# A state-space stage run by sequence inside a stage of indirect gathers

## The reference

```python
sx, ix = top_k(sim[0], 8); sy, iy = top_k(sim[1], 8)         # 128 keys each
scores, pk = top_k((sx[..., :, None] + sy[..., None, :]).reshape(..., 64), 8)
indices = take_along_axis(ix[..., :, None] * 128 + iy[..., None, :], pk)
w = silu(einsum('btd,bthkd->bthk', x, down_embed[indices])) * softmax(scores)
y = einsum('bthk,bthkd->btd', w, up_embed[indices])
y = y + (silu(x @ Wg.T) * (x @ Wu.T)) @ Wd.T
```

```python
u, v = split(x @ in_proj_w + in_proj_b)
v = depthwise_conv3(silu(v)) + conv_b
h_t = a * h_{t-1} + ssm_b * v_t;  y_t = ssm_c * h_t + ssm_d * v_t      # a = sigmoid(logit_a)
out = (u * silu(y)) @ out_proj_w + out_proj_b
part = layernorm(out + x) * ln_w + ln_b
```

## Time and profile before

| what | value |
|---|---|
| median of 3 runs | 3108.74 us (3105.13 to 3114.55) |
| the profiled execution: span | 3106.5 us; no other time is given for it |
| gather stage | from 1879 to 2595 us, gathers from 1898.4 to 2577 |
| its layer norm | 2595 to 2617 us |
| state-space stage with both norms | 2617 to 2730 us |
| busy over the span | PE 75%, DVE 52%, ACT 31%, POOL 25% |

### The profile page before, as it was taken

How to read it: one execution, slowest core, us unless ns; L and a number is a source line. 1 busy time by engine, 2 the same in 40 slices (tenths; PEclk the granted TensorE clock), 3 DMA queues, 4 the chain that set the end, 5 groups by cost and what they waited for, 6 DMA issues and landing times. The chain is left out here.

```text
span 3106.5 us, 37880 instructions
## 1 busy us (share of the span) xinstructions
PE 2320.2 (75%) x13729; PEld 1493.0 (48%) x13729; DVE 1607.0 (52%) x4352; ACT 963.3 (31%) x1784; POOL 787.0 (25%) x755
## 2 busy tenths in 40 slices
PE   6877699888777655485677674877777877689786
PEld 3544378735443432462244333666666664237332
DVE  3754300067545657246374666655665544533486
ACT  0132222210241322132114463443334334424343
POOL 1000200041001006451000004777777771000000
PEclk9999699989998877796899897988889889899898
DMA  7200244337006142553500106222222221000000
GB/s 183 63 21 2 99 149 172 143 85 177 11 18 176 38 159 108 182 179 128 94 5 23 69 1 152 66 55 56 53 55 58 62 53 37 0 29 1 1 0 27
DMA packets 126828, 232.20 MB, mean 75 GB/s; under 512 B 38777, under 2 KB 76537, under 8 KB 122560
## 3 DMA queue, kind: packets, MB, share of 16 engines
q1 hardware_dynamic: 73552, 125.12, 14.2%
q0 software_dynamic: 51952, 100.65, 11.0%
q10 hardware_dynamic: 1152, 4.19, 0.3%
HBM read 245.59 MB, written 66.72 MB: 101 GB/s over the span
## 5 line engine op out<-in xcount | busy, mean ns | idle before, releaser
L3192 POOL DMA_INDIRECT L2f_G<-in_L2f_table,L2f_idx x512 | 523.7, 1023 | 288.7 <-issue 155.2
L3249 PE MATMUL psum<-L2f_G,L2f_diag 128*128 128x256 f32 x1024 | 304.4, 463 | 168.8 <-ACT L2f_diag L3319 168.8
L3249 PEld LDWEIGHTS psum<-L2f_G,L2f_diag 128*128 128x128 f32 x1024 | 235.9, 236 | 234.8 <-ACT L2f_diag L3319 192.0
L3427 DVE CUSTOM_DVE_ANT_0 L2f_junk<-L2f_G,L2f_X 128x256 bf16<-128x256 f32 x512 | 182.8, 421 | 254.0 <-DMA L2f_G<-in_L2f_table,L2f_idx 253.9
L3319 ACT ACTIVATE L2f_diag<-const,L2f_actd 128x128 f32<-128x128 f32 x528 | 161.1, 388 | 24.2 <-DVE L2f_actd L3441 24.2
L1191 PE MATMUL psum<-constb 128*128 128x256 bf16 x512 | 81.0, 282 | 96.8 <-ACT L1a_PT L1358 24.6
L2669 POOL DMA_INDIRECT picks_x<-L1f_rows,L1f_put x64 | 71.0, 1109 | 242.1 <-ACT L1f_rows L2759 223.2
L3226 PE MATMUL psum<-xT,L2f_mw 128*128 128x256 f32 x512 | 123.2, 385 | 0.0
L3312 ACT ACTIVATE L2f_actd<-L2f_dots 128x9 f32<-128x9 f32 (+1 forms) x64 | 13.5, 211 | 316.3 <-DVE L2f_dots L3427 316.3
L1358 ACT ACTIVATE L1a_PT<-psum 128x1536 f32<-128x1536 f32 x32 | 46.4, 1450 | 205.5 <-PE psum L1326 205.5
L1191 PEld LDWEIGHTS psum<-constb 128*128 128x128 bf16 x512 | 41.0, 99 | 142.2 <-ACT L1a_PT L1358 32.9
(11 more groups left out here) (689 smaller groups left out, 4882.8 us busy)
## 6 DMA issues: line engine op xcount, KB each, us to landing
L1f_we<-in_L1f_w SPq DMA_DIRECT2D x32, 384.0 KB, 8.2
picks_x<-zeros SPq DMA_DIRECT2D x16, 544.0 KB, 9.1
L1f_xe<-picks_x SPq DMA_DIRECT2D x32, 272.0 KB, 2.9
picks_y<-zeros SPq DMA_DIRECT2D x16, 512.0 KB, 6.4
L2f_G<-in_L2f_table,L2f_idx POOLq DMA_INDIRECT x512, 2.8
slots_x<-zeros POOLq DMA_DIRECT2D x8, 512.0 KB, 7.6
L1f_wb<-in_L2x_w SPq DMA_DIRECT2D x1, 4096.0 KB, 12.2
L1f_g<-picks_y ACTq DMA_DIRECT2D x8, 512.0 KB, 11.9
```

The source lines that it names most:

```text
L3192: nc.gpsimd.indirect_dma_start(out=G[:, h, k, :], out_offset=None, in_=ins["L2f_table"], in_offset=bass.IndirectOffsetOnAxis(ap=IDX[:, t, ...
L3249: mm = nc.tensor.matmul(ps[:, MIX_BANK + t % 2, 0:D], diag[:, i % 2, k, :], row[:, D:2 * D], start=(h == 0 and k == 0), stop=(h == HEADS - ...
L3427: e = V.tensor_tensor_reduce(out=junk[:, k, :], in0=row[:, 0:D], in1=X[:, t % 3, :], scale=1.0, scalar=0.0, op0=ALU.mult, op1=ALU.add, acc ...
```

## The change

The stage L3a is no longer a stage. peer_ssm_stage takes peer_stage's place and runs it within the steps:

- The layer norm after L2f, the state-space part, its own norm and the layer norm after it are done for one sequence of 256 tokens at a time, in eight hops d = 0 to 7 (ssm_at). PE and ACT do hop d of sequence m at the end of step 9 + 8m + d, DVE one step later. The loop has END = 74 steps; the last ten have no gathers. Hop 0 subtracts the mean, 1 ends the L2f norm, 2 is conv, scan and skip, 3 the gate, 4 the output projection and residual, 5 the own norm, 6 and 7 the layer norm. All hops share PSUM bank 7; the dense MLP's down projection moves into one bank.
- Of a step's eight picks, the last two (OWN = 6) are weighted and summed on DVE into `rest`; ACT makes two diagonals and PE two matmuls fewer. keep, now on DVE, adds `rest` to the mix. POOL's wait before a head has a second part, pk_scaled.
- ACT's tables are named by hand (tables()) and loaded before the wait of the function that needs them.
- The squares of the norms are taken on DVE in place of ACT; the state-space input is projected in two hops (v in 2, u in 3); the skip product is on DVE in place of ACT.
- In best_pairs four additions become one; in experts 16 instructions of 64 elements become two of 512.
- ACT waits at the stage's start for the L3a weights and takes the sigmoid of logit_a. The weights of L3x are loaded by SP once pk_used shows the picks of step 60.

```diff
-STAGES = [..., "L2f", "L3a", "L3x", "L3f"]
+STAGES = [..., "L2f", "L3x", "L3f"]
...
+    def turned(i):
+        return [(k, row) for k, row in enumerate(rows(i)) if not OWN <= k < TOPK]
+    def ssm_at(i):
+        m, d = divmod(i - PER - 1, PER)
+        return (m, d) if 0 <= m < B else (0, None)
...
# POOL, before the gathers of a head
     pool.wait_ge(s["pk_used"].sem, s["pk_used"].at((t - 1) * HEADS + h + 1))
+    pool.wait_ge(s["pk_scaled"].sem, s["pk_scaled"].at((t - 1) * HEADS + h + 1))
...
# PE, a step
-                for i in range(STEPS):
+                for i in range(END):
                     up(i + 1); queries(t + 2); picks(i); down(i - 1); similar(t + 2); turn_back(t - 1)
+                    ssm(i)
...
# ACT
+                def inverse_root(done):
+                    tables(LOGS)
+                    act.wait_ge(s["var_ready"].sem, s["var_ready"].at(done))
+                    link(nc.scalar.activation(root, ps[:, SSM, 0:CW], ACT.Ln, bias=c.eps))
+                    link(nc.scalar.activation(root, root, ACT.Exp, scale=-0.5))
+                    nc.scalar.activation(square, root, ACT.Square).then_inc(s["root_ready"].sem, 1)
...
# DVE
+                def scaled(i):
+                    for k in range(OWN, TOPK):
+                        row, by = rows(i)[k][:, D:2 * D], act_d[:, i % 2, k:k + 1]
+                        if h == 0 and k == OWN:
+                            e = VE.tensor_scalar(rest[:, :], row, by, None, ALU.mult)
+                        else:
+                            e = VE.scalar_tensor_tensor(rest[:, :], row, by, rest[:, :], ALU.mult, ALU.add)
...
+                    if d == 2:
+                        for k in range(DH):
+                            link(VE.scalar_tensor_tensor(L[:, k, :], V[:, k, 1:1 + SEQ], cw(1), L[:, k, :], ALU.mult, ALU.add))
+                            link(VE.scalar_tensor_tensor(L[:, k, :], V[:, k, 2:2 + SEQ], cw(2), L[:, k, :], ALU.mult, ALU.add))
+                            VE.tensor_tensor_scan(H[:, k, :], decay[:, k:k + 1].broadcast_to([P, SEQ]), L[:, k, :], 0.0, ALU.mult, ALU.add)
+                            link(VE.tensor_scalar(S[:, k, :], L[:, k, :], wa["sd"][:, k:k + 1], None, ALU.mult))
+                            VE.scalar_tensor_tensor(S[:, k, :], H[:, k, :], both[:, k:k + 1], S[:, k, :], ALU.mult, ALU.add)
...
# DVE, a step
                     dot(i); add_mix(t - 1); add_dense(t // 2 - 1); gated(i); weighted(i)
+                    keep(t - 1); scaled(i)
+                    ssm(i - 1)
                     (best_keys, best_pairs, experts)[h - 1](t + 2)
...
-        norm_stage(nc, c, name, acc)
```

More of the change, by code:

```diff
@@ L3163, in peer_stage, with sa @@
         h_ = sb("h", [P, 3, CW])
-        mix = sb("mix", [P, 1, D])
+        mix, rest = sb("mix", [P, 1, D]), sb("rest", [P, D])
         got = ("got_head0", "got_head1", "got_head2", "got_head3")
+        def sa(nm, shape):
+            return work.enter_context(nc.sbuf_tensor(f"L3a_{nm}", shape, F32))
+        V = sa("V", [P, DH, SEQ + 2])
+        L, H, S, U = (sa(k, [P, DH, SEQ]) for k in ("L", "H", "S", "U"))
+        decay, both, mid = sa("a", [P, DH]), sa("both", [P, DH]), sa("mid", [P, DH + 1])
+        root, square, step = V[:, 0, 1:1 + SEQ], V[:, 1, 1:1 + SEQ], S[:, 0, :]
         def tile(t):
@@ L3215, in similar @@
                             rows = slice(half * RD, (half + 1) * RD)
-                            mm = nc.tensor.matmul(ps[:, SIM_BANK + half, tile(o_)], q[rows, o_, :],
+                            mm = nc.tensor.matmul(ps[:, SIM + half, tile(o_)], q[rows, o_, :],
                                                   w["keys"][rows, o_ * KEYS:(o_ + 1) * KEYS], start=True, stop=True)
@@ L3255, in turn_back, with average @@
                     for j in range(DH):
-                        mm = nc.tensor.transpose(ps[:, MIX_BANK + t % 2, tile(j)], mix[:, 0, tile(j)], c.ident)
+                        mm = nc.tensor.transpose(ps[:, MIX + t % 2, tile(j)], mix[:, 0, tile(j)], c.ident)
                     mm.then_inc(s["pk_yturn"].sem, 1)
+                def average(y):
+                    for j in range(DH):
+                        mm = nc.tensor.matmul(ps[:, SSM, 0:CW], c.mean, y[:, j, :], start=(j == 0), stop=(j == DH - 1))
+                    return mm
@@ L3328, in _ @@
+                c.wait_weights(act, "L3a")
+                nc.scalar.activation(decay[:, :], wa["la"], ACT.Sigmoid).then_inc(s["decay"].sem, 1)
                 for t in range(2):
@@ L3340, in _ @@
                         evac_queries(t + 2)
-                    if h == 0 and t:
-                        keep(t - 1)
                     if h == 0 and t + 2 < NT:
@@ L3458, in _ @@
                     experts(t)
-                for i in range(STEPS):
+                for i in range(END):
                     t, h = divmod(i, HEADS)
-                    dot(i)
-                    if h == 1 and t:
+                    if i < STEPS:
+                        dot(i)
+                    if h == 1 and 0 < t <= NT:
                         add_mix(t - 1)
@@ L3465, in _ @@
                             add_dense(t // 2 - 1)
-                    gated(i)
-                    weighted(i)
+                    if i < STEPS:
+                        gated(i)
+                        weighted(i)
+                    if h == 0 and 0 < t <= NT:
+                        keep(t - 1)
+                    if i < STEPS:
+                        scaled(i)
+                    ssm(i - 1)
                     if t + 2 < NT and h:
                         (best_keys, best_pairs, experts)[h - 1](t + 2)
-                add_mix(NT - 1)
-                add_dense(NT // 2 - 1)
+                    if i == 0:
+                        prepare()
                 s["dve_chain"].base += link.n
@@ L3518, in program @@
         run = STAGES
-        packed = [n for n in run if n in PACK]
+        packed = PACKED
         c.w, order = {}, {}
```

558 lines of the change are left out of this document (238 added, 320 removed).

## The result

The changed kernel takes 3026.14 us (median of 4 runs, 3024.55 to 3033.36), the kernel before 3110.72 beside it on the same chip (4 runs, 3105.13 to 3114.55): ratio 0.9732, 95% interval [0.971, 0.9754]. 3030 was forecast, with 3008 to 3050 as its own range. The profiled execution has a span of 3022.7 us, 83.8 less than before.

The account below looks back on a forecast made before the run. POOL's chain of gathers was taken to bound the gather stage. 3106.5 - 94 - 2 + 1 + 13 + 3 = 3027.5 us of span, so 3030 forecast (73%), own range 3008 to 3050, whole range 3006 to 3072.

Parts of the forecast that it names:

- the tail: After the last picks, before the cross-attention stage: 44.5 us in place of 138.5, so -94 us; over 55 would show it wrong.
- the spacing of the gathers: Sign, in the gather steps: gathers stand 1.33 to 1.36 us apart if the forecast is right.
- VectorE's wait for rows: Sign, in the gather steps: VectorE's wait for gathered rows falls from 254 us to 20 to 100.
- The hops' term: In the tail, eight hops in series: 38 us, with 33.5 at full clock and 42 as ends.
- the lead-in: Start of the tail: keep, then hops 6 and 7 of sequence 6, with hand-overs: 6.5 us.
- The table load in hop 5: In the tail, ScalarE's shift of xT and table load ahead of the root: 1.1 us not hidden by TensorE's matmul.
- The gathers: Gather steps: 129 us of added two-input VectorE work slows POOL's gathers by 0.10 us per us, +13 us.
- Rival 2: Gather steps: POOL and VectorE exclude each other, added two-input work costs +129 instead of +13, kernel 3146 us; chance 5%.
- VectorE's room: Gather steps: VectorE goes from 52 to 74 us a sequence, plus 3 to 8 of waits: 77 to 82 of 85.
- Rival 1: At weighted() after hops 1, 3, 5, 7: VectorE becomes the bound, 91 us a sequence against 85, kernel 3062 us; chance 22%.
- The start: Stage start: ScalarE's wait for L3a weights and sigmoid table +2, first tile's index arithmetic 1 shorter: +1 us in sum.
- Step 63: Last gather step: +3 us for ending later behind the gathers, and 2 us earlier for fewer matmuls and diagonals.

Follow-up runs that it names:

- Experiments 6 to 8: Changed kernel plus three idle TensorE matmuls before tail waits, 3021.55 us; then ScalarE's table loaded early too, 3023.35; then idle matmul counts fitted, 3150.33 on another chip.
- experiments 2 and 4: Changed kernel plus two unused 512-element VectorE instructions a step: two-input tensor_tensor, 3066.86 us; tensor_scalar, 3043.47 us.
- experiments 2 and 3: Changed kernel plus two unused 512-element VectorE instructions a step: two-input tensor_tensor, 3066.86 us; one-input reductions, 3065.01 us.
- experiment 5: Changed kernel with all eight picks of a step on TensorE: 3047.29 us, ratio 0.9778; the changed kernel beside it 3029.67 us.
- experiment 11: Changed kernel with TensorE running all eight picks' matmuls while ScalarE builds six diagonals: 3173.46 us, on a chip where the kernel before takes 3233.66.
- experiment 8: Changed kernel with early table load and idle TensorE matmuls fitted to each tail wait: 3150.33 us, ratio 0.9761, where the kernel before takes 3233.66.

## Why the prediction was right, step by step

The span was to shrink by 79 us and shrank by 83.8. The mechanism held; that the sum came so near is in part luck, since the tail missed by +3.8 us and the other terms by -8.6 together, of which 1.9 lie ahead of the stage. Of the signs, the spacing of the gathers (1.35 us) was in its range, VectorE's wait for rows (102) just above its 20 to 100, the last stretch 48.2 and not 45, and the first gather earlier, not later.

**The tail.** -94 was forecast, -90.2 came. That the norm, the state-space stage and its norms leave the path, and a lead-in and eight hops stay, held. The hops' term was mis-sized: 38 us, midway between 33.5 at full clock and 42 at 1.2 GHz, and it was 40.5 (2606.3 to 2646.8), the lead-in 7.7 for 6.5. On the path TensorE has four averages of 2.05 to 2.08 us, one of 1.13, and 3.78 and 3.52 for projection and output product; by these times all stood at 1.2 GHz but the one of 1.13 and a part of the output product. Experiments 6 to 8 show that this is the clock and nothing else in those matmuls, since the same instructions take 1.10 to 1.13 and 1.99 behind idle matmuls. The table load in hop 5, of which 1.1 us were taken as on the path, had 1.04 on it (2633.83 less 2632.79, the average's end).

**The gathers.** +13 forecast, +10.4 came; the price of 0.10 us for each us of two-input work was of the right size: 0.05 to 0.09 from the two picks, 0.13 from the two-input instructions against the one-input ones, and 8.3 us of the gathers' busy time for the hops' some 80 us (1 sequence's 18 less the picks' 6.7, times seven), 0.10. The forecast took the hops times eight, though those of sequence 7 lie behind the last gather: 1 us too much. It chose 0.10 among 0, 0.06 and 0.2, and that choice was a guess from one pair of gathers. Rival 2 falls with this: it needed 0.7. The Trainium skill ("SBUF - State Buffer", section "Who interferes with whom") has the loser block fully, lists tensor_scalar among the operations that can enter a two-port mode, and adds that a probe saw tensor_copy but not tensor_tensor stall such DMAs; experiments 2 and 4 show about a tenth of the time with tensor_tensor, and with tensor_scalar nothing above one-input work.

**VectorE's room.** 74 us a sequence and 3 to 8 of waits were forecast. Both came: in each of the sequences 2 to 6, from first dots to first dots, less the waits for rows and for weights, VectorE is taken for 73.9 to 74.1 us, and it waits 2.7 to 5.0 for the weights. Sequence 0, in whose steps no hop runs, has 60.0, so that the mean over all eight (577 us from first to last dots less 102, waits of 3.3 in it) is 69. Rival 1, VectorE as bound at 3062, was not far: experiments 2 and 3 reach 3067 and 3065 with 11 us more a sequence, and show its place, weighted(), and one of its signs, POOL waiting for picks.

**The start.** +1 forecast, -0.7 came. The sigmoid's table was loaded at 1877.21, ahead of the wait for the weights, not behind: the queries were copied 4.66 us after the stage began, for 4.26 before, +0.4 instead of +2.

**Step 63.** +3 for a later end and -2 for fewer matmuls were taken; -1.1 came. The last picks end 14.8 us after the last gather's start before the change, 12.9 with the hops left out, 13.8 and 13.4 with them: the 2 us for fewer matmuls were right, and of the 3 the hops cost 0.5 to 0.9.

**What the forecast didn't see** is that the two picks on VectorE were needed. It priced them as 8.8 us of VectorE's time a sequence and a part of POOL's 13, and their relief only as 2 us at the end. But its own round (10.3 us from dots to dots with six diagonals and picks of 2.8) gives 11.7 with eight (2.45 for 1.9, and 3.7 for 2.8), which is more than a step's 10.6. I made the same omission in the expectation of experiment 5. The forecast's total doesn't suffer from it, because it forecast the kernel with six; it was right on a point that it hadn't worked out.

## What to carry to other kernels

Where an engine runs ahead through buffers, a consumer that is too slow doesn't show in the producer's rate until the buffers are full: measure the backlog (producer's last item to consumer's last) stage by stage, and not the waits alone. Work that is put into in-order queues lengthens the round from engine to engine, and a step can be full by its round while no engine is full by its busy share; moving two picks of eight from ScalarE and TensorE to VectorE, which had room, was worth 18 us here, for up to 5 us more of the gathers' busy time. A serial tail of short matmuls can stand mostly at TensorE's lower clock: filling its waits with idle matmuls, and loading one table earlier, took it from 48.2 to 41.8 us, of which the table load is 1.0.

## What the runs showed of the hardware

- In the changed kernel's tail TensorE stood at 1.2 GHz after waits of 3.2 and 5.0 us, and at the next average after each (2.05 to 2.08 us); once, in experiment 11, it stood at 2.4 GHz after a wait of 3.2 us (1.10). In experiment 8, behind idle matmuls and waits of at most 1.9 us, the averages took 1.03 to 1.14 us, once 1.48. The Trainium skill ("TensorE: Matmul & The Clock Gate", section "What's actually happening") has two levels, 1.2 and 2.4 GHz, and the trace agrees.
- 128 tensor_scalar instructions of 512 elements, median 0.42 us, left the gathers' busy time at 537.1 us, the same as 128 one-input reductions of 0.68 us (534.2 without either).
- One chip ran the kernel before in 3234 us, others in 3111 to 3121. In experiment 8's trace there, ScalarE takes up the dots 2.97 us after their end on the mean, 0.75 in the changed kernel elsewhere. The cause is not known.
